# Ranking tokens in the middle of the second half's convolutions, and the order of VectorE's work around it

## The reference

```
kv = einsum('bhil,bhjl->bijhl', k_, v_)          # k and v are the same ctx; 16 heads, 8 x 8 pairs
y = irfft(rfft(kv, 512) * rfft(ssm_kernel, 512))[..., :256]   # causal convolution along l
out = einsum('bijhl,bhil->bjhl', y + kv * D, layernorm(x))
x = x + tanh(g_xattn) * out
```

```
scores = sigmoid(xf @ w_router);  sfc = scores + corr_bias
topk_idx = top_k(where(group mask, sfc, -inf), 6)
routed = sum over the 6 of scores[e] * (silu(xf @ gate_w[e]) * (xf @ up_w[e])) @ down_w[e]
shared = silu(xf @ sh_gate_w) * (xf @ sh_up_w) @ sh_down_w
x = x + tanh(g_ffn) * (routed + shared)
```

## Time and profile before

| | |
|---|---|
| median of three runs | 587.53 us (586.39 to 587.93) |
| the profiled execution's own time | 592.33 us |
| its span in the trace | 590.2 us |
| PE, DVE, ACT, POOL busy | 443.5, 313.5, 200.1, 301.0 us |
| POOL idle ahead of a group's scatters | 75.6 us in three waits for DVE's line 703, 31.9 us in one wait for the landing of scatters |
| DVE idle ahead of line 697 | 17.6 us in four waits |
| share of the ending chain by engine | PE 67%, DVE 11%, issue 8%, DMA 5%, ACT 3%, POOL 2% |

### The profile page before, as it was taken

One profiled execution on the slowest core, in us unless ns is written; L12 is line 12 of the kernel. 1 busy time (PEld: TensorE's weight loads), 2 busy tenths in 40 slices (PEclk: granted clock), 3 DMA queues, 4 the chain that ended last, 5 costly groups with the idle time before them and its releaser, 6 DMA issues.

```text
span 590.2 us, 8581 instructions
## 1 busy us (share of the span) xinstructions
PE 443.5 (75%) x2098; PEld 334.7 (57%) x2098; DVE 313.5 (53%) x1141; ACT 200.1 (34%) x506; POOL 301.0 (51%) x240
## 2 busy tenths in 40 slices
PE   0181798789889666800599999999999999999700
PEld 0171676666767445500477777777777777777500
DVE  3679979966994804500344444444444444444227
ACT  2050633632553231100144444444444444444300
POOL 2800008865884760077066576666666666666610
PEclk9995889988969966955699999999999999999955
DMA  6999402221221498576356766666666666666488
GB/s 257 343 285 416 200 1 99 89 92 68 90 95 70 164 390 231 134 209 193 82 105 110 118 115 111 111 111 116 111 114 114 114 114 116 115 115 117 57 265 323
DMA packets 55706, 89.68 MB, mean 152 GB/s; under 512 B 6525, under 2 KB 49885, under 8 KB 55005
## 3 DMA queue, kind: packets, MB, share of 16 engines
q0 software_dynamic: 20160, 28.37, 28.4%
q1 hardware_dynamic: 35150, 49.33, 25.3%
q10 hardware_dynamic: 342, 11.35, 6.2%
HBM read 47.00 MB, written 42.03 MB: 151 GB/s over the span
## 4 chain that ended last, share of the span: by engine, by line
PE 67%; DVE 11%; issue 8%; DMA 5%; ACT 3%; POOL 2%; another core or an unknown queue 2%; SPq 1%; DVEq 0%; POOLq 0%; ACTq 0%
PE bank L1054 22%; PE bank L1073 15%; PE bank L943 6%; PE bank L914 4%; PE bank L1045 4%; PE bank L1064 4%; DVE arena L603 4%; PE bank L964 4%; PE bank L915 2%; DMA arena<-toeplitz 2%; PE bank L985 2%; DMA arena<-token_sums 2%; PE bank L934 2%; POOL work L354 1%
## 5 line engine op out<-in xcount | busy, mean ns | idle before, releaser
L383 POOL DMA_INDIRECT token_sums<-work,dest x108 | 168.3, 1558 | 113.8 <-ACT work L522 99.5
L1054 PE MATMUL bank<-wgu,work 128*128 x432 | 146.9, 463 | 0.0
L1073 PE MATMUL bank<-wd,work 88*128 x432 | 111.0, 379 | 0.0
L369 POOL DMA_INDIRECT expert_lists<-arena,slots x48 | 59.8, 1246 | 82.3 <-DVE slots L703 68.3
L865 DVE TENSOR_TENSOR work<-work,bank 128x176 f32<-128x176 f32 x108 | 36.4, 337 | 120.2 <-ACT work L507 120.2
L1054 PEld LDWEIGHTS bank<-wgu,work 128*128 128x128 f32 x432 | 74.1, 192 | 23.2 <-issue 0.5
L369 POOL DMA_INDIRECT expert_lists<-payload,slots x48 | 57.4, 1195 | 53.2 <-DMA expert_lists<-arena,slots 31.9
L507 ACT ACTIVATE work<-bank 128x176 f32<-128x176 f32 x108 | 34.2, 317 | 141.5 <-PE bank L1054 141.5
L847 DVE COPY work<-bank 128x256 f32<-128x256 f32 x108 | 45.8, 424 | 59.4 <-PE bank L1045 58.2
L1073 PEld LDWEIGHTS bank<-wd,work 88*128 88x128 f32 x432 | 73.3, 190 | 6.1 <-issue 0.2
L522 ACT ACTIVATE work<-bank,work 128x256 f32<-128x256 f32 x108 | 51.1, 473 | 53.6 <-issue 49.3
(11 more groups left out here) (137 smaller groups left out, 506.8 us busy)
## 6 DMA issues: line engine op xcount, KB each, us to landing
payload<-expert_lists SPq DMA_DIRECT2D x108, 144.5 KB
wgu<-w_gu ACTq DMA_DIRECT2D x1, 6688.0 KB
arena<-token_sums SPq DMA_DIRECT2D x12, 512.0 KB, 8.3
expert_lists<-blank SPq DMA_DIRECT2D x1, 4768.5 KB, 26.7
wgu<-w_gu SPq DMA_DIRECT2D x1, 4576.0 KB, 17.5
token_sums<-blank SPq DMA_DIRECT2D x1, 4480.0 KB, 36.5
wd<-w_down ACTq DMA_DIRECT2D x1, 2992.0 KB
arena<-toeplitz SPq DMA_DIRECT2D x1, 2048.0 KB, 12.1
```

What stands on the lines that cost most here:

```text
L369: nc.gpsimd.indirect_dma_start(lists, bass.IndirectOffsetOnAxis(ap=slots[:, g % 2, b, k:k + 1], axis=0), pay[g % 2][:, b, :], None).then_i ...
L383: nc.gpsimd.indirect_dma_start(sums, bass.IndirectOffsetOnAxis(ap=dest[:, t % NPICK:t % NPICK + 1], axis=0), y_row(t), None, compute_op=AL ...
L1054: last = nc.tensor.matmul(bank[2 + t % 2][:, 0:2 * M], xT_half(t, k), wgu[:, bass.ds(e * WGU_E + k * 2 * M, 2 * M)], start=(k == 0), stop= ...
L1073: last = nc.tensor.matmul(bank[6 + t % 2][:, 0:L], hT_half(t, c), wd[:, bass.ds(e * WD_E + c * L, L)], start=(c == 0), stop=(c == 1))
```

## The change

PE's rank moves from behind `convolve(1)` to between its fourth and fifth head in groups 0 to 2, and `shared_hT(g, 0)` moves behind the last head. On DVE, `sum_pairs(0)` is split: the 32-wide add stays ahead of `choose()`, and the 16-wide and the 8-wide one (`sum_rest(0)`) stand behind `shared_times(0)`, ahead of `place_rows`. `shared_times(1)` moves from ahead of `times_q(1)` into it, between its fifth and sixth multiply (between d = 2 and d = 3). No instruction is added or removed.

```diff
-                def times_q(s):
+                def times_q(s, between=None):
...
                     for d in range(DH):
                         y = win(arena, CONV_AT + s * CONV_H + PAIR_AT[d], [[NP, CELLS], [1, DH - d]])
+                        if d == 3 and between:
+                            between()
...
-                def sum_pairs(s):
-
-                    cell = DH * DH
-                    for n in (cell // 2, cell // 4):
-                        low, high = (win(arena, Z_AT + o, [[cell, CELLS], [1, n]]) for o in (0, n))
-                        link(nc.vector.tensor_tensor(low, low, high, ALU.add))
+                def halve(n):
+
+                    low, high = (win(arena, Z_AT + o, [[cell, CELLS], [1, n]]) for o in (0, n))
+                    link(nc.vector.tensor_tensor(low, low, high, ALU.add))
+
+                cell = DH * DH
+
+                def sum_rest(s):
+
+                    halve(cell // 4)
...
                 if attend:
                     times_q(0)
-                    sum_pairs(0)
+                    halve(cell // 2)
+                    if not route:
+                        sum_rest(0)
                 if route:
                     chosen = choose()
                     shared_times(0)
+                    if attend:
+                        sum_rest(0)
                     place_rows(chosen)
-                    shared_times(1)
+                    if not attend:
+                        shared_times(1)
...
                 if attend:
-                    times_q(1)
+                    times_q(1, (lambda: shared_times(1)) if route else None)
                     if route:
                         shared_times(2)
-                    sum_pairs(1)
+                    halve(cell // 2)
+                    sum_rest(1)
...
-                if attend:
-                    convolve(1)
+                if attend and route:
+                    convolve(1, range(HALF // 2))
+                elif attend:
+                    convolve(1, range(HALF))
                 if route:
-                    shared_hT(g, 0)
+                    if not attend:
+                        shared_hT(g, 0)
...
                         last.then_inc(counts_ready, 1)
+                    if attend:
+                        convolve(1, range(HALF // 2, HALF))
+                        shared_hT(g, 0)
                     shared_up(1)
```

More of the change, by code:

```diff
@@ L903, in group, with convolve @@
             def group(g, attend, route):
-                def convolve(s):
+                def convolve(s, heads):
                     pe.wait_ge(products_ready, (g + 1) * 2 + s + 1)
-                    for hh in range(HALF):
+                    for hh in heads:
                         h = s * HALF + hh
@@ L974, in group @@
                                    xn_ready, lambda p: (g + 1) * 2 + p + 1, 5, qT_ready)
-                    convolve(0)
+                    convolve(0, range(HALF))
                 if route and g:
```

## The result

Measured alternately on one chip, the kernel before has a median of 586.96 us (585.89 to 587.93, 4 runs) and the changed one 580.31 us (578.41 to 582.13, 4 runs): a ratio of 0.988, 95% interval 0.9857 to 0.9902, so 6.65 us faster. The profiled execution of the changed kernel took 579.97 us.

What follows compares the result with a forecast made beforehand. The prediction took the landing of group 2's scatters, for which POOL's group 3 waits, as the gate. Gains of 2.9 + 1.8 = 4.7 us off the median of 587.53 us gave 582.8 us, range 578.5 to 586.0 us.

Steps and rivals of the forecast that it cites:

- Where the gate is: Ahead of PE's tiles: POOL's group 3 scatters wait, idle for 31.86 us, until group 2's scatters have landed.
- the two things that set it: For group 2's landing: first, when ACT issues the late weights; second, how many group 2 scatters are then queued.
- Term 1: PE and DVE end group 2 earlier: PE's 0.96 us waits in groups 0 to 2 vanish, weights issued 2.9 us earlier.
- the gain carries over: After PE's removed wait, the chain through PE and ACT keeps the 0.96 us a group, waiting for DVE nowhere long.
- Term 2: Group 2's places known earlier: its scatters lead the weights by 2 to 4 us more; two fewer queued give 1.8 us.
- The upper bound of 1.8 us: Most a queued group 2 scatter could be worth: 18 us of POOL's wait for ten scatters and the remaining weights.
- the near 8 us: Whole gain if DMA engines alternate queues packet by packet, each scatter worth nearer its upper bound; instead of 4.7 us.
- The stops in the heads: PE and ACT stops in the last heads before the rank, some 2 us; expected to fall behind or on the rank.
- first rival: At the DMA engines: only the weights' earlier issue counts, scatters cost nothing; 2.9 us gain, 584.6 us; chance 0.18.
- The adds that cost nothing: On DVE, the two moved adds take 2.0 us within a wait of 2.27 us or more.
- The mask: It must be ready when PE reaches the rank: margin 0.7 us in group 0, about 1 us in groups 1 and 2.
- the slower rival: PE stops at the mask within the heads and drops to the lower clock; 595.7 us; chance 0.06.

Runs made afterwards that it cites:

- pool_held: Changed kernel, with POOL starting group 2's scatters only when DVE has done shared_times(1); 581.91 us, ratio 0.9899 to the kernel before.
- rank_late: Changed kernel with PE's rank and shared_hT(g, 0) behind all eight heads again, DVE's new order kept; 581.37 us, ratio 0.9969 to the kernel before.
- times_ahead: Changed kernel with shared_times(1) ahead of times_q(1) again; 582.23 us, ratio 0.9983 to the kernel before.
- before_third: The kernel before, unchanged, profiled a third time, on chip 2; median 582.5 us.
- after_again: The changed kernel, unedited, measured again on chip 2; 580.3 us, ratio 0.9947 to the kernel before.
- before_again: The kernel before, unchanged, profiled a second time, on chip 3; median 586.4 us.
- sums_ahead: Changed kernel with both remaining adds of the first half ahead of choose() again; 579.75 us, ratio 0.9937 to the kernel before.
- before_shift: Kernel before, with POOL holding group 0's scatters until the third product of the shared expert is done; 583.71 us, ratio 1.0008 to the kernel before.
- after_shift: Changed kernel, with POOL holding scatters of groups 0 and 1 until the shared expert's second product is done; 581.29 us, ratio 0.9958 to the kernel before.
- wd_later: Changed kernel with the second late load, 2992 KB of down weights, issued at the very end; 596.87 us, ratio 1.0116 to the kernel before.
- after: The changed kernel in its first measurement, on chip 1; 580.3 us, ratio 0.988 to the kernel before.
- wd_mid: Changed kernel with 2992 KB of down weights issued in group 3 once group 2's scatters have landed; 579.93 us, ratio 0.9945 to the kernel before.

## Why the prediction was right, and where it was off

The forecast was 582.8 us with a range of 578.5 to 586.0; measured were 580.31 us on the first chip, and 2.4 to 2.8 us less than before on two others. Point by point:

- **Where the gate is** was right: POOL's group 3 follows the weights' issue by 43.7 to 45.7 us in every kernel that keeps the late loads where they were. pool_held and rank_late moved the second of the two things that set it, times_ahead the first.
- **Term 1**, 2.9 us for three waits of PE's line 953 for DVE, was right in its place, and near in size by two things that the prediction didn't have. The waits are in all profiles of the kernel before and in times_ahead, and in none of the changed kernel. Without its wait, the way from the second half's heads of group 0 to the next first half takes 22.9 us instead of 24.1, so a wait is worth 1.2 us rather than 0.96. But "the gain carries over" was not quite so: the stretch behind it in group 1 takes 0.3 to 1.2 us longer at a mean clock of 0.76 instead of 0.83, with no stop at the mask, which was the only place where the prediction looked for a loss of clock. Put back alone, the three waits cost 1.97 us in time, and 2.2 us at the weights' issue.
- **Term 2**, "two of them give 1.8 us", was too large. POOL's group 2 starts 19.2 us ahead of the weights before and 20.7 to 20.9 us after, so one scatter fewer stands behind them, not two. The lead grew by less than the 2 to 4 us of the forecast. A scatter is worth 0.1 to 0.6 us between 9 and 13, and nothing that shows below 9. The lag itself fell by 1.2 us on chip 1 (44.8 to 43.7) and by 0.3 us on chip 2 (44.3 to 44.0). These falls are no larger than the spread between profiles with the same number behind. My price of 0.89 us came from the rate of one window. The upper bound of 1.8 us was further off still. So was the near 8 us that the prediction worked out by the rule of the Trainium skill (page "DMA: Bandwidth & Descriptors", section "Queues, rings and completion order").
- **The stops in the heads** were in the prediction ("no visible cause"), but only as 2 us on the way to the places. The step that was off is this: I took them for part of every execution that would "fall behind the rank". In the changed kernel they are not there. They stood ahead of the weights' issue too, and so belonged in term 1. In the three profiles of the kernel before they are 5.6, 2.0 and 0 us (the 0.5 us of the table are one head at the lower clock).
- **The sum**: on chip 2 it is 142.3 - 138.8 = 3.5 us at the weights (before_third against after_again): 1.2 to 1.3 us in each of the three groups (3.8 us in all), 0.5 us for the head at the lower clock and 0.1 us elsewhere, less 0.9 us that the lower clock takes back in group 1. The first tile is 3.6 us earlier, the median 2.8 us. Where the kernel before takes 587 to 588 us, its profiles have 2.0 us of stops or more. before_again (chip 3) against the changed kernel (chip 1) gives 224.8 - 218.2 = 6.6 us at the first tile, of which 5.3 us stand at the weights and 1.6 us in the lag, less 0.3 us behind it; the time says 6.65 us, but the comparison crosses chips. So the gain is above the forecast of 4.7 us where the kernel before has the stops, and below it where it has none. The forecast time was met on the first chip with a gain that the prediction had not counted, and the 2.4 to 2.8 us of chips 2 and 4 are as near to its first rival (only the bulk's start counts, 2.9 us) as to anything. That the first time came out within its range is in part luck.
- **The first profile** was taken 4.8 us above the median, and 5.9 us above before_again: 3.6 us more of stops and a start-up 2.1 us longer (56.64 against 54.50 us to the first product). To take that difference off both sides alike was sound for the start-up and wrong for the stops, of which the changed kernel's profiles show none.
- **The adds that cost nothing**: nothing in sums_ahead speaks against it. **The mask**: no wait of PE for it in any profile (it is there 0.6 to 0.9 us early in group 0 of the changed kernel, 0.7 us forecast); the slower rival had no start. DVE's new wait for the scores is 1.40 us in group 1 and 1.74 us in group 2, as forecast.

**Open**: what stops ACT's copies for 1 to 2.5 us in the heads of the kernel before, on chip 1 and chip 3. The end of POOL's run within the heads isn't enough for it (before_third, before_shift, after_shift, pool_held, wd_later). That the new order removes the stops rests on three profiles there (after, pool_held, wd_later: none) against two of the kernel before (both have them). That is argued, not shown, and by which instruction it does so wasn't found.

## What to carry to other kernels

Put work with slack (adds, multiplies) ahead of a product that waits for another engine, and see who waits behind the product: here five multiplies moved ahead of one wait gave 2 us. Look at what stands behind the gate before removing it: here (wd_mid) POOL went on 18 us sooner, the wait came back behind its last scatter, and nothing was gained. A wait removed from PE can come back in part as a lower clock in the next stretch. And profile the kernel before more than once, on more than one chip, before a stop "without a cause" is counted as fixed.

## What the runs showed of the hardware that was not expected

- A queued scatter of 148 KB behind 9.7 MB of weights costs 0.1 to 0.6 us from the tenth to the thirteenth and nothing that shows before; issued beside 5.6 MB of loads, a last scatter takes 20.04 us to land instead of 2.6 to 2.8.
- Five profiles in which PE stops for 0.95 us at the end of group 0 hold a mean granted clock of 0.83 or 0.84 in the next first half of the convolutions; nine without that stop hold 0.76 there and take 0.3 to 1.2 us longer.
- POOL issues 24 scatters in 29.2 us while DVE is idle but for 0.5 us (237.33 to 266.49), and in 33.6 us (before_shift, group 0) to 38.9 us (84.37 to 123.31 in the changed kernel, group 0) while DVE is busy for nine tenths of the time.
- The same kernel before is at 583 us on chips 2 and 4 and at 587 to 588 us on chips 1 and 3, while the changed one stays within 0.4 us in three measurements (chips 1, 2 and 4).
